# Attention sums taken in groups 9 and 1, and key-difference steps behind the second maxima

## The reference, cut to what matters

```
q, k, v = (proj(Wq), proj(Wk), proj(Wv))              # 2 x 16 heads, 2048 x 64 each
scores = jnp.einsum('bhqd,bhkd->bhqk', q, k) + bias    # 2048 x 2048 for each head
attn = jax.nn.softmax(scores, axis=-1)
ctx = jnp.einsum('bhqk,bhkd->bhqd', attn, v)
```

## Time and profile before

| | |
|---|---|
| median of 3 runs | 3970.04 us |
| the profiled execution | 3972.34 us |
| its span, first to last instruction | 3970.6 us |
| mean granted TensorE clock | 0.977 of full speed |
| TensorE busy | 3727.9 us, 94% |
| VectorE busy | 2466.4 us, 62% |
| ScalarE busy | 2004.6 us, 50% |
| GpSimd busy | 2681.1 us, 68% |
| heads 0 to 30 | 263.08 to 2895.58 us, 31 heads |

### The profile page before, as it was taken

One profiled execution on the slowest core, in us unless ns is written; L12 is line 12 of the kernel. 1 busy time (PEld: TensorE's weight loads), 2 busy tenths in 40 slices (PEclk: granted clock), 3 DMA queues, 4 the chain that ended last, 5 costly groups with the idle time before them and its releaser, 6 DMA issues. The chain is left out here.

```text
span 3970.6 us, 64135 instructions
## 1 busy us (share of the span) xinstructions
PE 3727.9 (94%) x21277; PEld 2216.2 (56%) x21277; DVE 2466.4 (62%) x3356; ACT 2004.6 (50%) x3452; POOL 2681.1 (68%) x1402
## 2 busy tenths in 40 slices
PE   8989999999999989999999999999997999997899
PEld 7754444444444444444444444444446888885377
DVE  3466666666666656666666666666635777775632
ACT  3335555555555555555555555555553555553232
POOL 1128888888888878888988888889893343430010
PEclk9989999999999999999999999999998999998999
DMA  7652222432223452222332222332312333335710
GB/s 221 162 120 63 66 64 71 103 75 69 64 64 81 101 153 64 69 64 67 93 90 66 68 64 67 98 84 65 105 36 88 100 106 103 104 116 174 262 46 22
DMA packets 368370, 366.99 MB, mean 92 GB/s; under 512 B 189339, under 2 KB 261531, under 8 KB 362776
## 3 DMA queue, kind: packets, MB, share of 16 engines
q1 hardware_dynamic: 299064, 336.50, 31.6%
q10 hardware_dynamic: 67168, 20.98, 2.2%
q0 software_dynamic: 1920, 6.29, 0.5%
HBM read 142.64 MB, written 89.70 MB: 59 GB/s over the span
## 5 line engine op out<-in xcount | busy, mean ns | idle before, releaser
L354 POOL TENSOR_TENSOR acc<-acc,probs 128x1024 f32<-128x1024 f32 x894 | 2126.4, 2379 | 306.9 <-ACT probs L814 189.3
L939 DVE TENSOR_REDUCE maxes<-ps 128x2 f32<-128x1024 f32 x1024 | 1253.2, 1225 | 607.6 <-PE ps L610 596.7
L817 ACT ACTIVATE probs<-ps,far_bias 128x1024 f32<-128x1024 f32 (+7 forms) x1280 | 997.4, 819 | 795.4 <-DVE near_s L956 546.0
L641 PE MATMUL ps<-probs,v_head 128*64 128x512 f32 x4096 | 1002.1, 610 | 8.9 <-ACT ctx_out L800 6.9
L629 PE MATMUL ps<-stacks 64*128 64x512 f32 x6144 | 825.7, 398 | 1.8 <-ACT probs L814 1.8
L629 PEld LDWEIGHTS ps<-stacks 64*128 64x128 f32 x6144 | 591.0, 188 | 126.9 <-ACT probs L814 7.9
L610 PE MATMUL ps<-stacks 64*128 64x512 f32 x2048 | 508.0, 494 | 142.4 <-DVE maxes L939 56.9
L610 PEld LDWEIGHTS ps<-stacks 64*128 64x128 f32 x2048 | 194.5, 187 | 700.0 <-DVE maxes L939 464.3
L641 PEld LDWEIGHTS ps<-probs,v_head 128*64 128x64 f32 x4096 | 251.0, 137 | 463.0 <-issue 450.9
L956 DVE TENSOR_TENSOR near_s<-ps,near_bias 128x384 f32<-128x384 f32 (+2 forms) x576 | 265.8, 491 | 58.4 <-PE ps L629 55.3
L962 DVE TENSOR_TENSOR c_q<-ps,c_q 64x512 fp32r<-64x512 f32 x128 | 87.5, 684 | 311.2 <-ACT c_q L773 311.2
(11 more groups left out here) (278 smaller groups left out, 4515.4 us busy)
## 6 DMA issues: line engine op xcount, KB each, us to landing
stacks<-c_q SPq DMA_DIRECT2D x128, 256.0 KB, 4.3
stacks<-c_d SPq DMA_DIRECT2D x64, 512.0 KB, 6.9
stacks<-c_k SPq DMA_DIRECT2D x32, 768.0 KB, 5.5
stacks<-c_k SPq DMA_DIRECT2D x64, 384.0 KB, 7.0
scr_v<-probs ACTq DMA_DIRECT2D x32, 512.0 KB, 4.1
v_head<-scr_v SPq DMA_DIRECT2D x32, 512.0 KB, 8.5
scr_ctx<-ctx_out SPq DMA_DIRECT2D x128, 128.0 KB, 2.3
both_ctx<-scr_ctx SPq DMA_DIRECT2D x32, 512.0 KB, 4.0
```

The lines of the kernel that those rows point to most:

```text
L354: pool.tensor_tensor(acc[:, qb, :], acc[:, qb, :], pr, ALU.add).then_inc(s["summed"], 1)
L641: mm = pe.matmul(ps[64 * half:64 * half + 64, PV, :], v_head[:, side, kt, :], probs[:, st % PT_RING, half * 512:(half + 1) * 512], start=k ...
L817: ins = act.activation(probs[:, st % PT_RING, a:z], sc[:, a:z], ACT.Exp, bias=bias)
L939: dve.tensor_reduce(maxes[:, qt:qt + HALF_GROUPS // 2 + 1:HALF_GROUPS // 2, first_chunk + pair], ps[:, bank:bank + 2, :], AX.X, ALU.max).t ...
```

## The change

Three tables of groups get other numbers. The sum of half 0 is taken in group 9 in place of 13, that of half 1 in group 1 of the next head in place of 5; the reciprocals follow in groups 10 and 3, the contexts at steps 25 and 11. On SP the `divisors` of half 0 move ahead of `guard(n+1, 0)`. The projection waits for the sums' copies at blocks 0 and 2, since these are the first that use the bank after the sums. On DVE `step` and `step_lo` stand behind the second maximum of their group. From line 506 on, line numbers after the change are one higher (two higher in lines 496 to 503).

```diff
-SUM_GROUPS = {13: 0, 5: 1}
-RECIP_GROUPS = {14: 0, 6: 1}
-CONTEXT_STEPS = {31: 0, 15: 1}
+SUM_GROUPS = {9: 0, 1: 1}
+RECIP_GROUPS = {10: 0, 3: 1}
+CONTEXT_STEPS = {25: 0, 11: 1}
...
                 if h_weights is not None:
                     xn_block(1, reload)
+                if own:
+                    divisors(n, 0)
                 if nxt:
                     guard(n + 1, 1 - side, 0)
...
                 if own:
-                    divisors(n, 0)
                     store_ctx(n, 0)
...
-                    if tb == 1:
+                    if tb == 0:
                         past(pe, s["sum_out"], 2 * (m - 2))
-                    if tb == 3:
+                    if tb == 2:
                         past(pe, s["sum_out"], 2 * (m - 2) + 1)
...
+                    if has_max(n, g):
+                        largest(n, side, g, 1)
                     if prep and g in STEP_GROUPS:
                         step(n + 2, STEP_GROUPS[g])
                     if lowered:
                         step_lo(*lowered)
-                    if has_max(n, g):
-                        largest(n, side, g, 1)
```

## The result

The kernel after takes 4109.81 us (median of 4 runs, 4104.88 to 4112.47) against 3970.53 us for the kernel before (the median of four runs now): a ratio of 1.0351, with an interval of 1.0333 to 1.0368. It is 139 us slower; the forecast was 36 us slower. The direction was right, the size was not, and the time lies outside the range that was given.

The account below looks back on a forecast made before the run. TensorE was taken to set the pace, save where VectorE puts a step between maxima or SP is late. 3972.3 + 160 losses - 124 gains = 4008 us profiled, 4006 as the median; range 3945 to 4048.

Parts of the forecast that it names:

- gains (fill, its clock, steps, context copies): TensorE's waits and slow products removed: 42.7 for the fill, 12 clock, 62 steps, 6.9 context copies, 124 us in all.
- wait in group 4, 27 heads: VectorE's reciprocal of half 1 waits for late part, delaying TensorE in group 4: 126 us over 27 heads.
- clock behind it, same heads: Lower TensorE clock after the 27 stalls at the reciprocal of half 1: 15 us more.
- heads 13, 14, 30 (with their clock; net of what goes in 14): Same stall in special heads: 11 us in head 13, -1 in head 14, 9 in head 30.
- Odd heads, 3.6 us: TensorE's loss in group 4 per odd head, with the fill starting 4.3 us before the head's start.
- `part`, 3.6 us from its first issue to its landing: On SP's queue behind the guard's read back: four transfers take 2.5 us, the last lands 1.7 us after issue.
- The clock, a share of 10 in 23: Ten of 23 fill waits had a 1.3 us clock fall behind them; this share put 15 us on 27 stalls.
- the rival that the clock costs more groups: TensorE stays at 1.2 GHz beyond one group after stalls; groups 4 and 5 cost 1.3 us more: 4042 us, chance 0.15.
- longer in even heads: Sign of being right: the reciprocal's wait for part, 90 to 160 us in about 29 heads, is longer in even heads.
- VectorE comes no earlier than part: Part lands before about 24 us into both kinds of heads, so the stall is smaller: 3936 us, chance 0.15.
- Gains and losses meet: The stall in group 4 is about 1.3 us a head shorter, leaving no change within 8 us: 3970 us, chance 0.13.
- The steps gain nothing: TensorE waits as long for the first maximum behind the moved step; the 62 us are lost: 4068 us, chance 0.07.

Follow-up runs that it names:

- recip5_ctx13: Kernel after with half 1's reciprocal at the end of group 5 instead of 3 and its context product at step 13: 3829.36 us, 0.9637 of before.
- the seventh experiment: Kernel after with a loop body of four heads in place of two on every engine: 4103.0 us, 1.0328 of before.
- the fourth experiment: Kernel after with half 1's reciprocal in group 5, context product at step 13: 3829.36 us; the same with steps back between the two maxima: 3897.03 us.

## Why the prediction was wrong

By the trace of the kernel after, taken at 4110.6 us against the 3972.3 of before, the terms stand so (us):

| term | predicted | measured |
|---|---|---|
| gains (fill, its clock, steps, context copies) | 124 | 136 |
| wait in group 4, 27 heads | 126 | 191 |
| clock behind it, same heads | 15 | 60 |
| heads 13, 14, 30 (with their clock; net of what goes in 14) | 19 | 23 |

The wait and the clock are read from the second maximum product of group 4 and the one behind it in each head, less their lengths in a plain group; the gains are not measured by themselves but the rest of 138.3. 23 is 12.8 in head 13, 11.9 in head 14 less the 13 that go there, and 10.9 in head 30. The runs give the same: `recip5_ctx13` has every gain and next to no stall, and lies 143 us below before and 280 below after.

**Right.** The gains, with the fill's wait gone and the steps worth their 62 us where nothing else is late. The place and chain of the new wait: fill, guard's write, read back, `part`, reciprocal, maximum, product. The start of the fill in even heads and its 23 us of draining there. Heads 13, 14 and 30.

**The step that failed** is the size of the stall ("TensorE loses 5.8 us in even heads and 3.6 in odd ones") and the share of the clock beside it.

- *Odd heads, 3.6 us.* Measured 7.3, which is 52 us more over 14 heads. The fill starts at T - 3.7, not T - 4.3, and drains in 25.1 us, not 23. The start is later because the last group ahead of an odd head, 6.13 us on the mean before, lasts 5.62 after the change (5.70 with the sums alone moved, 6.13 with the steps alone); I had used its length of before. That group is also some 7 us of the larger gains. For the 25.1, I took the 23 from heads whose fill began at T + 4.1 and moved the start without asking what else moves bytes at the new time. Instruction packets do, as the seventh experiment's comparison suggests.
- *`part`, 3.6 us from its first issue to its landing.* Measured 4.5 in both kinds of heads. My 2.5 and 1.7 us came from a place where nothing is ahead on the queue; here the guard's read back is right ahead, though no run shows that this is the reason. (23.1, 2.0 and 3.6 also make 28.7, not 28.5.) In even heads this is nearly all of the difference between 5.8 and 6.9.
- *The clock, a share of 10 in 23.* That share was of waits of 1.9 us for the fill (42.7 over 22). Behind waits of 5.8 to 11.4 us, 7.1 on the mean, it fell in all 30 heads (a granted clock of 0.50 to 0.59 in the stretch behind), and it cost 2.2 us each (1.9 in group 4 on the mean, 0.3 in group 5), not 1.3 us in ten of 23. The 1.3 us was read from head 18: before the change group 3 ran below full clock in 11 heads, for 1.1 us each on the mean. So the rival that the clock costs more groups was right in kind; by the prediction's own figure it alone gives 4042. The Trainium skill (TensorE: Matmul & The Clock Gate, "Loop structure matters more than you think") warns of a long wait for DMA in every turn of a loop, behind which the matmuls run cold; the row with 0.50 behind the wait in head 16 agrees.

Together: 65 us of waits, 45 of clock, 4 of the three heads, less 12 of larger gains, is the 102 us between 4008 and 4110. Of the signs that the prediction named, "longer in even heads" came out the other way: the reciprocal waits longer in odd ones.

**The rivals.** *VectorE comes no earlier than part* needed `part` by T + 24; it lands at T + 27 to 28. Neither kind of head comes near it. The runs that took the guard out of the way, or the reciprocal two groups on, made the rival's case by hand, and came out faster as it said. *Gains and losses meet* needed a shorter stall than forecast, and it was longer. *The steps gain nothing* is refuted by 68 us in the fourth experiment.

## What to carry to other kernels

When an instruction moves ahead on an in-order engine, work out when its data lands on the queue as it will be then, with all that is queued and all that loads at that time; a drain time read at another place of the loop is not the drain time here. A wait that recurs in every turn is priced as its length plus the slow products behind it. A change that gains in six places and loses in one is not to be dropped but mended: here two groups in one table and two steps in another turned 3.5% slower into 3.6% faster.

## What the runs showed of the hardware that was not expected

- A queue of its own does not bring a small transfer past a large one: 1.7 us alone, 5 to 9 us in most cases beside the fill.
- Four DMA issues held ACT for 5.52 us in head 16 while SP issued the fill and the transfers behind it, and for 2.4 us in head 31, which has no fill; SP needs 2.5 us for the same four.
- Instruction packets of 16 KB, 0.96 us each, go with a fill that drains in 25 us in place of 23; an earlier fill meets them, a later one does not. That they are the cause is not shown.
- A wait of some 7 us was followed by a granted clock of 0.50 to 0.59 in each of 30 heads, that is, by 1.2 GHz for most of the stretch behind it, at a cost of 2.2 us on the mean; waits of 2.9 us on the mean were followed by a lower clock in 21 of 30.
